# A four-layer kernel on one core: in its first layer, gated attention is interleaved with norms, routing, places and marks, at stated paces

## The reference

```python
    x = L0_attn_x
    xn = _layernorm(x, axis=-1)
    x = x + _L0_attn_ref(xn, ...) + _L0_ffn_ref(xn, L0_ffn_Wr, L0_ffn_W1, L0_ffn_W2, L0_ffn_W3)
    xn = _layernorm(x, axis=-1)
    x = x + _L1_attn_ref(xn, ...) + _L1_ffn_ref(xn, ...)
...
    return x
```

```python
    def _L0_attn_ref(x, Wq, Wk, Wv, Wg, Wgk1, Wgk2, bgk2, Wo, g_norm_weight):
...
            def step(S, inp):
                q_t, k_t, v_t, g_t = inp
                S = S * jnp.exp(g_t)[:, None] + k_t[:, None] * v_t[None, :]
                return (S, q_t @ S)
...
        gk = jax.nn.log_sigmoid(x @ Wgk1 @ Wgk2 + bgk2) / GATE_LOGIT_NORMALIZER
...
        g = (x @ Wg).reshape(b, n, h, dv)
        o = o * jax.lax.rsqrt(jnp.mean(o * o, axis=-1, keepdims=True) + EPS) * g_norm_weight
        o = o * (g * jax.nn.sigmoid(g))
        return o.reshape(b, n, h * dv) @ Wo

    def _L0_ffn_ref(x, Wr, W1, W2, W3):
...
        gate_logits = xf @ Wr
        w, idx = jax.lax.top_k(gate_logits, TOP_K)
        w = jax.nn.softmax(w, axis=-1)
...
        h = jnp.einsum('nc,ech->neh', xf, W1)
        g = jnp.einsum('nc,ech->neh', xf, W3)
        y = jnp.einsum('neh,ehc->nec', jax.nn.silu(h) * g, W2)
        out = jnp.einsum('nec,ne->nc', y, comb)
```

## Time and profile before

| what | value |
|---|---|
| median of 3 runs | 3849.35 us |
| lowest and highest | 3842.29 and 3860.38 us |
| profiled execution: its span, first to last instruction | 3867.5 us |
| PE busy | 3519.2 us (91%), 16468 passes |
| DVE, ACT, POOL busy | 2473.4, 1730.0, 1164.8 us |
| share of the chain that ended last: PE | 66% |

### The profile page before, as it was taken

The page is one execution under the profiler, slowest core; times in us unless marked ns, Lnnn a source line. Parts: engine busy times, 40 slices in busy tenths (PEclk is TensorE's granted clock), DMA queues, the critical chain, the costliest instruction groups (busy, mean ns, idle before and its releaser), DMA issues.

```text
span 3867.5 us, 47778 instructions
## 1 busy us (share of the span) xinstructions
PE 3519.2 (91%) x16468; PEld 2089.1 (54%) x16468; DVE 2473.4 (64%) x6381; ACT 1730.0 (45%) x3237; POOL 1164.8 (30%) x1190
## 2 busy tenths in 40 slices
PE   8899999968898988989878999998899999999998
PEld 7677777734555545545546667676543333433332
DVE  4444443455788988889865443443568788678774
ACT  2234443322234423343344544443346666666667
POOL 0322222151355555555542322223211111011111
PEclk7799999988899999999989999999889899999999
DMA  3244445321466666666750000000101011111100
GB/s 109 73 165 168 177 180 180 128 66 71 136 204 193 216 211 194 197 204 197 212 187 3 0 1 1 1 1 9 38 20 31 20 23 34 31 34 27 32 18 23
DMA packets 107154, 368.87 MB, mean 95 GB/s; under 512 B 27248, under 2 KB 41088, under 8 KB 96928
## 3 DMA queue, kind: packets, MB, share of 16 engines
q0 software_dynamic: 57664, 302.82, 24.3%
q1 hardware_dynamic: 48160, 60.90, 5.6%
q10 hardware_dynamic: 1088, 2.10, 0.2%
HBM read 322.59 MB, written 17.69 MB: 88 GB/s over the span
## 4 chain that ended last, share of the span: by engine, by line
PE 66%; DVE 21%; ACT 6%; issue 4%; another core or an unknown queue 2%; POOL 1%; DMA 0%; POOLq 0%; DVEq 0%; SPq 0%; ACTq 0%
PE ps L184 51%; PE ps L2636 6%; DVE pm L2784 4%; PE ps L1507 2%; DVE mi L1642 2%; DVE gathB L1719 2%; DVE ps L2787 2%; DVE hacc L1682 2%; ACT P L2917 1%; PE ps L2126 1%; DVE mx L1638 1%; PE ps L556 1%; PE ps L581 1%; PE ps L546 1%
## 5 line engine op out<-in xcount | busy, mean ns | idle before, releaser
L2917 ACT ACTIVATE P<-ps 128x512 f32<-128x512 f32 (+3 forms) x1280 | 587.3, 548 | 214.1 <-PE ps L184 212.0
L2784 DVE TENSOR_REDUCE pm<-ps 128x1 f32<-128x512 f32 x768 | 484.6, 684 | 113.3 <-PE ps L184 113.0
L1860 POOL DMA_INDIRECT gathB<-in_tab,idx x256 | 282.9, 1105 | 357.6 <-PE ps L1507 287.4
L184 PE MATMUL ps<-QS,KS 49*128 49x512 f32 (+3 forms) x1280 | 333.8, 422 | 16.2 <-DVE pm L2784 12.6
L1860 POOL DMA_INDIRECT gathA<-in_tab,idx x256 | 268.7, 1049 | 203.2 <-DVE mx L1638 125.5
L184 PE MATMUL ps<-KS,QS 48*128 48x512 f32 (+3 forms) x1280 | 309.8, 430 | 16.0 <-DVE pm L2787 5.9
L2974 POOL TENSOR_SCALAR_AFFINE_SELECT P<-P 128x256 f32<-128x256 f32 x256 | 103.8, 409 | 709.9 <-ACT P L2917 709.0
L2636 PE MATMUL ps<-P,Va 128*32 128x512 f32 (+3 forms) x2560 | 309.7, 557 | 5.8 <-POOL P L2974 2.9
L184 PEld LDWEIGHTS ps<-QS,KS 49*128 49x128 f32 x1280 | 158.2, 190 | 225.0 <-DVE pm L2784 81.8
L184 PEld LDWEIGHTS ps<-KS,QS 48*128 48x128 f32 x1280 | 145.5, 191 | 212.8 <-DVE pm L2784 66.2
L2787 DVE CUSTOM_DVE_ANT_0 ps<-ps,past 128x128 f32<-128x128 f32 (+3 forms) x512 | 240.1, 515 | 26.6 <-PE ps L184 24.6
(11 more groups left out here) (390 smaller groups left out, 7002.8 us busy)
## 6 DMA issues: line engine op xcount, KB each, us to landing
ys_sorted<-moe SPq DMA_DIRECT2D x71, 128.0 KB
KS<-hi SPq DMA_DIRECT2D x256, 32.0 KB, 1.9
QS<-hi SPq DMA_DIRECT2D x256, 32.0 KB, 1.9
gathA<-in_tab,idx POOLq DMA_INDIRECT x256
gathB<-in_tab,idx POOLq DMA_INDIRECT x256
KS<-lo SPq DMA_DIRECT2D x128, 32.0 KB, 1.9
QS<-lo SPq DMA_DIRECT2D x128, 32.0 KB, 2.0
out<-xT SPq DMA_DIRECT2D x8, 512.0 KB, 3.2
```

The costliest lines, as they stand in the source:

```text
L184: m = pe.matmul(out, w, x, start=start and i == 0, stop=stop and i == len(pairs) - 1, skip_group_check=True)
L1860: pool.indirect_dma_start(out=(GA, GB)[half][:, h, :], out_offset=None, in_=d[f"tab{half}"], in_offset=bass.IndirectOffsetOnAxis(ap=idx[t ...
L2784: v = dve.tensor_reduce(m, p, AX.X, ALU.max)
L2917: act.activation(P_[:, hh, off:BW], psx.tile("s2", j, n, kt, pr, hh)[:, off:BW], ACT.Exp).then_inc(*psx.emptied(MN.act, "s2", j, n, kt, pr ...
```

## The change

Norms and routing are no longer a part of their own. They become the first steps of the experts' generator (`pe_moe`, `dve_moe`, `act_moe`), so that attention begins when the first block's norm is done, and runs beside the norms of the others, routing, places and marks. For that:

- the planner becomes `on_clock`, in which every step says by how much its clock advances. Attention starts at 5.2 with pace 1.0; the experts' steps have the paces 1.7 (10 steps of norms), 1.2 (16 pairs of routing), 4.0 (places), 1.6 (8 batches of marks), 0.8 (`BEFORE`), 0.63 (tiles, two steps each) and 1.1 (the rest: `AFTER` and combinations). The old planner had 1.0 against 1.4;
- `each_turn` does the norms with a yield after each turn, and `pe_route`, `act_route` and `dve_route` yield for each pair;
- the norm's root is taken by a logarithm and an exponential on ACT (`by_log`, `log_set`), in the table set that attention's decays use, and DVE's reciprocal goes;
- the squares move to the experts' buffer `moe`, since `QK` and `ob` are in use by then, and the bank `gates` moves from ring `psa` to ring `psf`, where it is kept.

The steps of attention, tiles and combinations are unchanged, and so are POOL's and SP's lists.

```diff
-        def pe_norm(pe, S, ps, key, src, ready, sq, rs):
+        def pe_norm(pe, S, ps, key, src, ready, sq, rs, by_log=False):
...
-            pe.wait_ge(*S.dve.has(*key, "rstd"))
+            pe.wait_ge(*(S.act if by_log else S.dve).has(*key, "rstd"))
...
-            dve.wait_ge(*S.act.has(*key, "var"))
-            dve.reciprocal(rs[:, 4:8], rs[:, 0:4]).then_inc(*S.dve.tick(*key, "rstd"))
+            if not by_log:
+                dve.wait_ge(*S.act.has(*key, "var"))
+                dve.reciprocal(rs[:, 4:8], rs[:, 0:4]).then_inc(*S.dve.tick(*key, "rstd"))
...
-            act.activation(rs[:, 0:4], p[:, 0:4], ACT.Sqrt, bias=epsc[:, 0:1]).then_inc(*ps.emptied(S.act, *key, "var"))
+            if log_set is None:
+                act.activation(rs[:, 0:4], p[:, 0:4], ACT.Sqrt, bias=epsc[:, 0:1]).then_inc(*ps.emptied(S.act, *key, "var"))
+            else:
+                log_set(act)
+                act.activation(rs[:, 0:4], p[:, 0:4], ACT.Ln, bias=epsc[:, 0:1]).then_inc(*ps.emptied(S.act, *key, "var"))
+                act.wait_ge(*S.act.has(*key, "var"))
+                act.activation(rs[:, 4:8], rs[:, 0:4], ACT.Exp, scale=-0.5).then_inc(*S.act.tick(*key, "rstd"))
...
+        def each_turn(gens):
+
+            for n in range(NB + 2):
+                if n < NB:
+                    next(gens[n])
+                if 0 < n <= NB:
+                    next(gens[n - 1])
+                if n > 1:
+                    for _ in gens[n - 2]:
+                        pass
+                yield
...
+            sqs = [part(i * 1024, 1024).rearrange("p (a b) -> p a b", a=2) for i in range(4)]
...
+            START, NORM, ROUTE, PLACES, MARKS, FIRST, TILE, LAST = 5.2, 1.7, 1.2, 4.0, 1.6, 0.8, 0.63, 1.1
+
+            def in_steps(gen, *paces):
+
+                for n, pace in paces:
+                    for _ in range(n):
+                        next(gen)
+                        yield pace
+                for _ in gen:
+                    yield paces[-1][1]
+
             def weave_layer(attn, experts):
-                weave((attn, 1.4), (experts, 1.0))
+                marks = 2 * NC // HOT
+                paces = ((NB + 2, NORM), (NC // 2, ROUTE), (1, PLACES), (marks, MARKS), (BEFORE, FIRST), (2 * TILES - 1, TILE), (1, LAST))
+                for _ in on_clock((START, in_steps(attn, (1, 1.0))), (0.0, in_steps(experts, *paces))):
+                    pass
...
                     if c % 8 == 0:
-                        gates = psa.fill("gate", c // 8)
-                        pe.wait_all(psa.freed("gate", c // 8))
+                        if c:
+                            psf.unkeep("gate", c // 8 - 1)
+                        gates = psf.fill("gate", c // 8, keep=True)
+                        pe.wait_all(psf.freed("gate", c // 8))
...
+                    yield
+                psf.unkeep("gate", NC // 8 - 1)
 
             def pe_moe(pe):
+                yield from each_turn([pe_norm(pe, LN, psf, (n,), both(xT, n), [XIN[n].has("x")], sqs[n % 4], rstd[n % 4], by_log=True)
+                                      for n in range(NB)])
+                yield from pe_route(pe)
...
             def pe(pe):
-                pe_all(pe)
-                pe_route(pe)
                 weave_layer(pe_attn(pe), pe_moe(pe))
```

More of the change, by code:

```diff
@@ L887, in dve_route @@
                     cs = range(8 * g, 8 * g + 8)
+                    for _ in range(4):
+                        yield
                     dve.wait_ge(*FF.pe.has("gate", g))
-                    dve.tensor_copy(lg[:, 8 * g:8 * g + 8, :].rearrange("p a b -> p (a b)"), psa.tile("gate", g)[:, 0:64]).then_inc(
-                        *psa.emptied(FF.dve, "gate", g))
+                    dve.tensor_copy(lg[:, 8 * g:8 * g + 8, :].rearrange("p a b -> p (a b)"), psf.tile("gate", g)[:, 0:64]).then_inc(
+                        *psf.emptied(FF.dve, "gate", g))
                     own()
@@ L973, in dve_moe @@
             def dve_moe(dve):
+                yield from each_turn([dve_norm(dve, LN, psf, (n,), both(xT, n), both(xn, n), [], rstd[n % 4], by_log=True)
+                                      for n in range(NB)])
+                yield from dve_route(dve)
                 dve_places(dve)
@@ L1182, in act @@
             def act(act):
-                act_all(act)
-                act_route(act)
                 table.clear()
```

13 lines of the change are left out of this document (7 added, 6 removed).

## The result

The changed kernel takes 3867.85 us (median of 20 runs, 3851.17 to 3881.51), the kernel before 3859.7 beside it (20 runs, 3841.86 to 3871.83): a ratio of 1.0031, with a 95% interval of 1.0017 to 1.0045. It is slower by 0.3%, 12 us: less than the 0.5% that the prediction can tell from no change, but the interval leaves out 1, and the gain of 0.56% is ruled out. A second comparison in a later job gave 1.0050 (1.0029 to 1.0072). One execution of a later variant, `s1_serial`, took 8221 us and is left out of its ratio. The profiled execution of the changed kernel has a span of 3849.1 us and is, at 3851.17, the shortest of the 20.

A forecast was written before the change was run, and what follows sets the result against it. The first layer's middle was taken as PE-bound, its two ends as slack. First tile 256, last tile 820, tail 108 and 3 gave 931 instead of 952.5; 21.5 off the median 3849.35 gave 3828 us, range 3795 to 3862.

The forecast's parts named there:

- Start to rank: loss 14: Norms and routing beside attention: 124 us of work plus 14 lost, 7 for input and 4 waiting for DVE; rank at 138.
- Places: a wait of 7: Behind the rank: PE waits 7 us, as attention's copies stand behind DVE's 8.0 us of places.
- Marks: PE waits 20: Eight batches of marks: PE waits 20 us in all for operands, against 24.0 in the kernel before.
- 4 us for the lock: Marks: DVE operations on two SBUF inputs slow beside POOL's product; 4 us for eight, half the worst case.
- Clock: I take 5: Places and marks: PE's lowered clock costs 5 us, with bounds 0 and 40.
- the lock and the chains: Before the first tile: 4 us for DVE slowed by POOL, 3 for attention chunks standing alone in PE, DVE, PE chains.
- rival 2: Half clock from places through marks: 40 us more, first tile at 296, time 3868; chance 0.12.
- 37 becomes 31, and 2: Tiles: loss falls from 37 to 31 us with five block ends instead of six, plus 2 for closer tiles.
- The tail: Behind the last tile: attention 37.9, a combination 1.8, 48 gathers 64.5, landing 2, last sum 2; 108 us, then 3.
- Rival 3: Nothing is gained: the tail takes all the front gives; break-even with last tile at 842, time 3849; chance 0.2.
- The baseline: Whole program: the profiled span, 3867.5 us, lies 18 above the runs' median 3849.35; the predicted difference was carried to that median.

The follow-up runs named there:

- s1_serial: The changed kernel with attention starting at 36.3 instead of 5.2, only when norms and routing are issued; ratio 1.0031 to the kernel before.
- r_after: The changed kernel, unchanged, profiled a second time in a later job; ratio 1.0050 to the kernel before.
- m1_lag: The changed kernel with PE's matmuls of each batch of marks one step later; ratio 0.9972 to the kernel before.
- r_before: The kernel before, unchanged, profiled once more in a later job; ratio 0.9996.
- g2_more: The changed kernel with PE's marks one step later, places in two steps, tile pace 0.56, combinations 6 steps behind the last tile; ratio 0.9879.
- m0_lag: The kernel before with only PE's matmuls of each batch of marks one step later; ratio 0.9955.
- c1_combine: The changed kernel with combinations of expert outputs 4 steps behind the last tile instead of 20; ratio 1.0022 to the kernel before.
- g1_half: The changed kernel with one gather per chunk instead of two, output incomplete; single run, layer 1 begins at 926.0 us.

## Why the prediction was wrong

The forecast was 3828 us and the result is 3867.85, 40 more. Of these, 10 are the baseline: its median of three, 3849.35, became 3859.7 over 20 runs. The other 30 are a gain of 21.5 that did not come and a loss of 8 in its place.

The waits and the chains that the prediction names are in the trace. The times of the stretches were set too low, in the first three terms in both profiles, in the tail in one of them:

| stretch | forecast | changed kernel | `r_after` |
|---|---|---|---|
| start to rank | 138 | 144.0 | 149.2 |
| rank to first tile | 118 | 126.4 | 126.2 |
| tiles | 564 | 570.8 | 568.3 |
| last tile to layer 1 | 111 | 114.8 | 106.5 |
| layer 1 begins | 931 | 956.0 | 950.2 |

- **"Start to rank: loss 14"** was 20 and 25. Input, 6.9, and the rank's wait, 3.3, are as forecast, and so is PE's idle time, 14.4. Missed was that PE is busy 5.6 us longer than the work priced from single rows, and that the clock can dip even here: `r_after` has it at the lower level for 10 us from 29 us on, which cost 5.
- **"Places: a wait of 7"** was 5.0. **"Marks: PE waits 20"** was 17.1 in six. Both right in mechanism and nearly in size. The **4 us for the lock** was too much: one operation of attention's was hit (1.62 us instead of 0.68), and two that read PSUM beside the product took 1.41 together, which is what the line takes elsewhere (0.74 each in the mean).
- **"Clock: I take 5"** is the step that failed in the front. From rank to first tile PE was busy 102.6 us, 40.6 of them at the lower clock by the profile's clock records, which costs half of that: 20 us instead of 5. In `m1_lag` PE is busy 89.3 us with the same work, so 13 of the 20 hang on the marks' waits; the marks' own matmuls have 7.8 of them (23.4 against 15.6). The waits, set at 34 with the lock and the chains, were 24, which hid part of it. The reasoning was "the gaps are short and dense work lies ahead", with the tiles' 0.99 for a guide. That figure is a mean over 587 us. The same trace, read right behind the single gaps of that stretch, has the lower clock at five block ends, behind waits of PE of 1.7 to 3.0 us. Two of the five, in the kernel before (columns as in the earlier trace rows):

```profile
240.20:243.40 3.20, 3.20 (x17) 3.20 (x17) 2.68 (x4) 1.49 (x3) 0.00 (x0) 0.50 0.86 355
346.00:349.30 3.30, 3.30 (x7) 2.00 (x6) 0.66 (x3) 1.38 (x3) 0.00 (x0) 0.50 0.01 2
```

The marks have six such gaps in 70 us, and so the mean falls: waits of 2.4, 2.7, 3.0 and 4.6 us stood directly ahead of four batches that took 2.8 to 3.7 us instead of 1.9, and one of 1.1 us ahead of a fifth, whose forerunner had waited 3.3. The Trainium skill's rule ("TensorE: Matmul & The Clock Gate", section "HAM oscillation — how this bites in real kernels"), that idle gaps bring the cold clock back each time, was argued away on the mean; the trace agrees with it in the marks and at the block ends, at a price of 20 us behind the rank, not rival 2's 40 on top of the 5.
- **Tiles: "37 becomes 31, and 2"**. The loss is 40 and 37. The waits are 22.2 us for five block ends (19.6 for six before): they didn't scale with the number of ends. The lower clock costs 11 (9 before). The other 7 are work that the rows price too low, and so are 9 of the 37 before.
- **The tail**, 111, was 114.8 and 106.5: the forecast lies between. The 8 us between the two are VectorE's last long waits, which `r_after` does not have.
- **Rival 3** ("nothing is gained", break-even with a last tile at 842) is what came: 841.2. It had 0.2. It should have had more: the forecast took the front's loss from 77 us to 53, where it fell to 68 in the first profiles and rose from 68 to 73 in the reruns.
- **The baseline.** The earlier trace rows was one execution, 21.6 us behind `r_before` in the first layer. Against that row the same sum would have given 931 against 931: no change. That the span stood 18 us above the median of the runs was seen and carried over as a constant; it was the warning.

Where the time went can be read from PE alone. Its idle time, and what the lower clock costs (half of the time that it was busy at that clock, by the profile's clock records), in us, before and after (the sums are of unrounded numbers):

| part of the layer | idle | lower clock | idle, reruns | lower clock, reruns |
|---|---|---|---|---|
| ahead of the first tile | 34, 38 | 38, 20 | 31, 37 | 32, 26 |
| tiles | 20, 21 | 9, 11 | 20, 21 | 10, 8 |
| behind the last tile | 47, 66 | 20, 14 | 36, 57 | 17, 14 |
| sum | 101, 125 | 67, 45 | 87, 116 | 60, 48 |

So the change did give back the lower clock of routing, and lost more than that in idle time, most of it behind the last tile. It moves 104 us of attention in front of the first tile, where the waits of the marks stay, since their operands are made in the same step, whatever stands beside. The attention that is spent there is missing behind the last tile, where 64 gathers of 1.3 us go on regardless: PE is busy 49 of 106 us there, 139 of 175 before. With the marks' part of PE one step later (26 us) and 61 us of work instead of 34 behind the last tile, the kernel with the early start is 1.2% faster than the kernel before (`g2_more`); some 0.45% of that the marks' step gives without it (`m0_lag`).

## What to carry to other kernels

Work put beside a chain covers it only if the consumer is listed a step behind the producer; in the same step the wait stays and takes the clock down with it. Read what a gap does to the clock right behind the gap: a mean over a long stretch (0.99 here) hides it. What fills a stall at one end is missing at the other: ask first what floor each end has (here 64 gathers), and share the filler by that. And take losses from two executions of the kernel before, when a profile's span lies off the median by as much as the effect.

## What the runs showed of the hardware that was not expected

- In the first profiles of the two kernels and in two of the four jobs that followed VectorE's last sums wait for PE's semaphore, up to 8.2 us in one wait in the changed kernel and up to 15.5 in `c1_combine`, in the tail only, while GpSimd issues gathers back to back: 13.9 us in the kernel before, 20.7 in the changed one, 12 to 23 in six variants (in `s1_serial` 7 us of such waits stand ahead of attention's operations instead). In all eight profiles of the two other jobs it is absent, with the same code and the same gathers. What holds it back stays open; `g1_half`, with half the gathers, lacked it among neighbours that had it.
- With the same instructions, the clock was at its lower level for 64 to 132 us behind 2700 us in these profiles, and rank came 144 to 155 us into the same front. Times of one kernel spread over 30 us, and go with the granted clock: 3851 us at 0.945 and 3881 at 0.935 in the changed kernel.
